# Second fold ahead of the third in the setup, and new orders for the last tiles of a cross-attention and FFN kernel

## The chip, the cores and the metric

One core of a Trainium2 chip. The metric is the device time of one execution in microseconds. The core has five engines, each with an instruction queue that is worked off in order: TensorE (PE), VectorE (DVE), ScalarE (ACT), GpSimd (POOL) and SyncE (SP), which here only issues transfers. They wait for each other by semaphores alone.

## The reference

x is 64 sequences of 64 tokens, width 256; ctx is 64 x 64 x 64. Everything is float32.

```python
q_big = einsum('bshk,hkq->bshq', (layernorm(x) @ Wq.T), w_kc_q)
kv_rope = kv_c * cos + rotate_half(kv_c) * sin
scores = (q_big . W_qr) . (kv_rope . W_kr)            # 16 heads, 64 wide
ctx_c = softmax(scores) @ kv_rope
x = x + (ctx_c . w_kc_kv) @ Wo.T
h = gelu(bitlinear(layernorm(x), w1))                 # 256 -> 1024
x = x + bitlinear(h, w2)                              # 1024 -> 256
```

bitlinear divides a row by its norm, rounds it to 8 bits by the row's largest absolute value, and multiplies it with a weight rounded to -1, 0 and 1.

## The kernel before, in words

The 4096 tokens are 32 tiles (`NT`) of 128 tokens. Setup folds the weights of queries and keys of each head into one 256 x 64 matrix: `first_fold` (W_qr with w_kc_q, PSUM banks 2 and 3, copied by `t_out`), `second_fold` (with W_kr, banks 4 and 5, `DB`, copied by `d_out`), `third_fold` (with Wq, copied by `at_out`), then `turn_a`, transposes whose result is split into `ah` and `al` by `a_hi` and `a_lo`. Each fold is made in two halves. `fold_out` does the same for w_kc_kv and Wo. Float32 products are made of three matmuls of high and low parts.

The main loop `for n in range(ENDS)` is a software pipeline written out for each engine: in step n TensorE makes `scores` of tile n, `queries` of later tiles, `shifts`, `contexts` of tile n-1, `project` of tile n-3, `up` (first FFN matmul) of tile n-7 and `down` (second) of tile n-10. VectorE finds the maxima (`quadrant_max`, `row_max`) and sums (`row_sum`, `row_inverse`) of the softmax, `divide`s the contexts, adds `residual`, and ends with `finish`. ScalarE does `exp`, `ctx_hi`, `gelu` and the squares. GpSimd does `ctx_lo`, `centre`, `x_round`, `g_round` and the small steps of the norms (`norms`, later `late_norm`). `g_round(t)` scales and rounds the 1024 gelus of a tile to integers in bfloat16 in two instructions (the first adds a large number, the second takes it away); `g_scale(t)` on VectorE gives its scale, and `turn_g(t)` on SP's queue transposes the result by DMA for `down`. `x_round` and `turn_x` do this for `up`. The inverses of the row sums go to DRAM and back, spread over partitions (`rinv_rows`, `rinv_spread`), before `divide` can use them.

After the loop, from about 355 us on, the order of the last tiles is written out by hand, one list for each engine. There `finish_late` adds the result into `xs` and `store_in_place` stores from it; `finish` writes to a buffer `yo` first. `g_round` of tiles 25, 26, 28 and 31 is done by VectorE (`DVE_LATE`), the others by GpSimd. `free_bank` makes TensorE wait until a bank that `USES` deals out in turn has been read.

## Time and profile before

| | us |
|---|---|
| three runs | 409.55, 409.83, 412.76 |
| median | 409.83 |
| profiled execution: its time | 411.0 |
| profiled execution: its span | 409.2 |
| TensorE busy in the span | 377.2 (92%) |
| VectorE, GpSimd, ScalarE busy | 319.1, 273.1, 260.4 |
| mean granted TensorE clock | 0.982 of full speed |

The span runs from the first to the last instruction of the profiled execution; its own time is 1.8 us longer and 1.2 us above the median. Instants below are microseconds from the span's start.

### The profile page before, as it was taken

The page shows a single profiled execution, that of the slowest core. Times are in us where ns is not written, and L with a number is a line of the kernel's source. Part 1 is how long each engine was busy: PE and PEld are TensorE (multiplying, and loading weights), DVE is VectorE, ACT ScalarE, POOL GpSimd, SP SyncE. Part 2 cuts the span into 40 slices and gives each one's busy share as a digit, 9 for nine tenths or more (in the row PEclk, how much of TensorE's full clock was granted, in tenths as well). Part 3 has the DMA queues.
Part 4 walks back from the last instruction along what each step waited for, and adds up shares of the span by engine and source line. Part 5 has one row for each costly group of instructions (what it writes and reads, how often), then busy time and mean ns, then how long its engine had stood idle before and what let it go on. Part 6 is the DMA issues. An engine that isn't in the chain of part 4 may idle for free.

```text
span 409.2 us, 8876 instructions
## 1 busy us (share of the span) xinstructions
PE 377.2 (92%) x2870; PEld 270.5 (66%) x2870; DVE 319.1 (78%) x669; ACT 260.4 (64%) x480; POOL 273.1 (67%) x406
## 2 busy tenths in 40 slices
PE   7898898988999999999999999999999999888764
PEld 6577656666766677777776767676767676554522
DVE  0453868779979898878797888788888888898983
ACT  1245365443586868686868686868686868667850
POOL 1026807476576787878785868686777757687882
PEclk9999999999999999999999999999999999998967
...
GB/s 201 354 377 167 106 157 128 133 129 120 104 19 84 63 105 81 117 81 99 100 93 105 78 120 71 126 67 131 69 131 66 87 111 114 103 110 148 76 96 136
DMA packets 65549, 48.75 MB, mean 119 GB/s; under 512 B 50400, under 2 KB 55904, under 8 KB 65120
## 3 DMA queue, kind: packets, MB, share of 16 engines
...
## 4 chain that ended last, share of the span: by engine, by line
POOL 47%; issue 27%; PE 9%; DMA 8%; DVE 6%; SPq 2%; POOLq 1%; ACT 0%; DVEq 0%
POOL cl L478 12%; POOL tq L504 6%; POOL qb L508 6%; POOL yc L489 3%; POOL xn L314 3%; POOL fw L527 3%; POOL xa L494 3%; DMA xs<-x 3%; DMA qt<-qb 2%; POOL xq L497 2%; PE hps L969 2%; POOL scl L534 2%; POOL rstd L216 2%; POOL fw L524 1%; PE ps L951 1%
## 5 line engine op out<-in xcount | busy, mean ns | idle before, releaser
L478 POOL TENSOR_TENSOR cl<-cr,ch 128x512 fp32r<-128x512 f32 x64 | 81.6, 1297 | 77.3 <-ACT ch L656 77.3
L640 ACT ACTIVATE qf<-ps 128x512 f32<-128x512 f32 x64 | 38.2, 596 | 71.0 <-PE ps L852 71.0
L850 PE MATMUL ps<-xh,ah 128*128 128x256 f32 x256 | 74.8, 292 | 0.3 <-ACT qf L640 0.3
L852 PE MATMUL ps<-xh,al 128*128 128x256 f32 x256 | 71.2, 278 | 0.0
L851 PE MATMUL ps<-xl,ah 128*128 128x256 f32 x256 | 71.2, 278 | 0.0
L915 PE MATMUL hps<-bh,ch 128*128 128x256 f32 x224 | 66.3, 296 | 0.0
L916 PE MATMUL hps<-bl,ch 128*128 128x256 f32 x224 | 62.6, 279 | 0.0
L917 PE MATMUL hps<-bh,cl 128*128 128x256 f32 x224 | 62.6, 279 | 0.0
L850 PEld LDWEIGHTS ps<-xh,ah 128*128 128x128 f32 x256 | 48.1, 188 | 17.1 <-issue 16.2
L656 ACT ACTIVATE ch<-cr 128x512 fp32r<-128x512 f32 x64 | 39.3, 632 | 24.0 <-DVE cr L1184 23.9
L1151 DVE TRANSPOSE_TENSOR_REDUCE red<-hps 128x16 f32<-128x512 f32 x64 | 41.8, 690 | 13.0 <-PE hps L867 12.9
L851 PEld LDWEIGHTS ps<-xl,ah 128*128 128x128 f32 x256 | 48.1, 188 | 0.0
L852 PEld LDWEIGHTS ps<-xh,al 128*128 128x128 f32 x256 | 48.1, 188 | 0.0
L682 ACT ACTIVATE g<-ps,scl 128x512 f32<-128x512 f32 x64 | 40.8, 682 | 10.1 <-PE ps L951 9.9
L1184 DVE TENSOR_TENSOR cr<-ps,rb 128x512 f32<-128x512 f32 x64 | 41.3, 685 | 6.9 <-issue 4.3
L951 PE MATMUL ps<-w1q,xqt 128*128 128x512 bf16 x128 | 37.5, 396 | 7.5 <-DMA xqt<-xq 6.1
L915 PEld LDWEIGHTS hps<-bh,ch 128*128 128x128 f32 x224 | 42.2, 189 | 1.4
L1158 DVE TRANSPOSE_TENSOR_REDUCE red<-pe 128x16 f32<-128x512 f32 x64 | 41.6, 688 | 1.8 <-ACT pe L651 1.8
L916 PEld LDWEIGHTS hps<-bl,ch 128*128 128x128 f32 x224 | 42.2, 188 | 0.3
L917 PEld LDWEIGHTS hps<-bh,cl 128*128 128x128 f32 x224 | 42.3, 189 | 0.0
L1206 DVE TENSOR_REDUCE amax<-g 128x1 f32<-128x1024 f32 x32 | 38.7, 1208 | 0.9 <-ACT g L682 0.8
L651 ACT ACTIVATE pe<-hps 128x512 f32<-128x512 f32 x64 | 34.6, 596 | 7.2 <-PE hps L895 7.2
...
## 6 DMA issues: line engine op xcount, KB each, us to landing
...
```

The lines of the kernel that those rows point to most:

```text
L478: pool.tensor_tensor(cl[:, u % 2, :, b * S:(b + 1) * S], cr[:, :, b * S:(b + 1) * S], ch[:, u % 2, :, b * S:(b + 1) * S].bitcast(F32), ALU ...
L682: act.activation(g[:, t % GB, 512 * half:512 * half + 512], turn_bank("h", t, half), ACT.Gelu, scale=hscale(scl, t)).then_inc(sem["gelu_do ...
L850: pe.matmul(o, ah[:, c, cols], xh[:, k % 2, c, :], start=(c == 0), stop=False)
L851: pe.matmul(o, ah[:, c, cols], xl[:, k % 2, c, :], start=False, stop=False)
L852: m = pe.matmul(o, al[:, c, cols], xh[:, k % 2, c, :], start=False, stop=(c == KC - 1))
L915: pe.matmul(O[:, 0:D], c_h, bh[:, hp, :], start=(hp == 0), stop=False)
L916: pe.matmul(O[:, 0:D], c_h, bl[:, hp, :], start=False, stop=False)
L917: m = pe.matmul(O[:, 0:D], c_l, bh[:, hp, :], start=False, stop=(hp == HP - 1))
L951: m = pe.matmul(turn_bank("h", t, half), xqt[:, t % 2, c, :], w1q[:, c, 512 * half:512 * half + 512], start=(c == 0), stop=(c == KC - 1))
L1151: dve.tensor_reduce(red[:, u % 2, 16 * b:16 * b + 16], SB[b].rearrange("p (k s) -> p k s", s=32), AX.X, ALU.max, apply_transpose=True).the ...
L1158: dve.tensor_reduce(red[:, (u + 1) % 2, 64 + 16 * b:80 + 16 * b], pe32[:, u % 2, b, :].rearrange("p (k s) -> p k s", s=32), AX.X, ALU.add, ...
L1184: dve.tensor_tensor(cr[:, :, b * S:(b + 1) * S], CB[b].rearrange("p (h s) -> p h s", s=S), rb[:, b, :].rearrange("p (h s) -> p h s", s=S), ...
```

## The change

1. Setup. TensorE makes the second half of `second_fold` ahead of the first half of `third_fold`, with three idle matmuls in front. `turn_a(0)` and `(1)` write banks 4 and 5 in place of the two that the queries use. VectorE copies `d_out(0)` before the statistics of the first x tiles, and converts `em` and takes the statistics of tiles 4 to 7 later. SP loads the second x part and `em_s` only once the first fold is made.
2. Stores. `finish` writes to `xs` too; `yo` is only room now.
3. End. No `g_round` is done by VectorE; tiles 25 and 31 go to ScalarE, and 26 and 28 to GpSimd besides its own six. `ctx_lo(31)` and `x_round(28)` move from GpSimd to VectorE, `centre(30)` from ScalarE to GpSimd. The lists of all five engines are written anew.

TensorE in the setup, before and after; `wkr_s,t_s` is the second fold, `wq_s,d_s` the third, `ident,at_s` the turning:

```order
L985 MATMUL ps<-wk_b,wqr_b 64x128 x2
L1007 MATMUL hps<-wq_s,d_s 64x256 x8
L326 MATMUL ps<-ident,xn 128x128 x4
L996 MATMUL hps<-wkr_s,t_s 128x64 x8
L1019 MATMUL ps<-ident,at_s 128x128 x8
```

```order
L996 MATMUL ps<-wk_b,wqr_b 64x128 x2
L986 MATMUL hps<-ones 128x128 x3
L1010 MATMUL hps<-wkr_s,t_s 128x64 x8
L1021 MATMUL hps<-wq_s,d_s 64x256 x8
L325 MATMUL ps<-ident,xn 128x128 x4
L1034 MATMUL hps<-ident,at_s 128x128 x8
```

The fold with W_kr has moved over the one with Wq and over the transposes of x.

VectorE at the start of the end (`cr<-ps,rb` is `divide`, `ri<-rs` is `row_inverse`, `amax<-g` is `g_max`), before and after:

```order
L1151 TENSOR_REDUCE red<-hps 128x16 x2
L1184 TENSOR_TENSOR cr<-ps,rb 128x8x64
L1164 TENSOR_REDUCE nmax<-hps 32x64
L1170 TENSOR_REDUCE rs<-hps 32x64
L1184 TENSOR_TENSOR cr<-ps,rb 128x8x64
L1189 SCALAR_TENSOR_TENSOR xs,xsum<-hps,xs 128x256
L1177 RECIPROCAL ri<-rs 32x64
```

```order
L1167 TENSOR_REDUCE red<-hps 128x16 x2
L1228 TENSOR_REDUCE amax<-g 128x1
L1180 TENSOR_REDUCE nmax<-hps 32x64
L1233 SCALAR_TENSOR_TENSOR gm<-amax,level 128x1
L1235 RECIPROCAL c_73<-gm 128x1
L1211 SCALAR_TENSOR_TENSOR xs,xsum<-hps,xs 128x256
L1186 TENSOR_REDUCE rs<-hps 32x64
L1216 TENSOR_REDUCE amax<-yc 128x1 x2
L1222 SCALAR_TENSOR_TENSOR gm<-amax,level 128x2
L1224 RECIPROCAL c_64<-gm 128x2
L1200 TENSOR_TENSOR cr<-ps,rb 128x8x64 x2
```

Both halves of `divide(29)` now stand behind nine instructions that stood behind them, or behind the first half.

ScalarE around its first `g_round`, after (`g,magic,c_73` and `qb<-g,magic`; `ch<-cr` is `ctx_hi(31)`):

```order
L679 ACTIVATE g<-ps,scl 128x512
L685 ACTIVATE sqj,stat<-g 128x1024 x2
L692 ACTIVATE g<-g,magic,c_73 128x1024
L696 ACTIVATE qb<-g,magic 128x1024
L653 ACTIVATE ch<-cr 128x8x64 x2
```

`ctx_hi(31)` stands behind the two new instructions of tile 25.

The diff, with most of the lists of the end left out:

```diff
-POOL_LATE = (22, 23, 24, 27, 29, 30)
-DVE_LATE = (25, 26, 28, 31)
+POOL_LATE = (22, 23, 24, 26, 27, 28, 29, 30)
+ACT_LATE = (25, 31)
...
-        yo = sb("yo", [P, 2, D], F32, at)
+        sb("room", [P, 2, D], F32, at)
...
-        USES = [("k", 0), ("e",), ("x", 0), ("a", 0), ("a", 1), ("q", 0, 0), ("q", 0, 1), ("x", 1), ("q", 0, 2), ("q", 0, 3)]
+        USES = [("k", 0), ("e",), ("x", 0), ("q", 0, 0), ("q", 0, 1), ("x", 1), ("q", 0, 2), ("q", 0, 3)]
...
-                if kind == "a":
-                    pe.wait_ge(sem["a_lo_done"], a + 1)
 
         FB, DB, AT = bank[2:4], bank[4:6], [bank[6], bank[7], bank[2], bank[3]]
 
         def turned_a(q):
-            return turn_bank("a", q) if q < 2 else (T, O)[q - 2]
+            return (DB[0], DB[1], T, O)[q]
...
-                    sp.dma_start(out[:, t, :], yo[:, t % 2, :]).then_inc(sem[f"out_stored{t % 2}"], 16)
-
-                def store_in_place(t):
-                    sp.wait_ge(sem["outputs"], t + 1)
...
+                sp.wait_ge(sem["t_made"], 2)
+                load_x(1)
                 for b in range(2):
                     sp.dma_start(em_s[64 * b:64 * b + 64, :], consts[b:b + 64, 2 * DC + b * P:2 * DC + (b + 1) * P]).then_inc(sem["em_loaded"], 16)
-                load_x(1)
-                sp.wait_ge(sem["t_made"], 2)
...
+                turn_x(26)
                 rinv_rows(30)
                 rinv_spread(30)
-                turn_x(26)
-                store_in_place(21)
-                turn_g(23)
+                store(21)
                 rinv_rows(31)
                 turn_x(27)
-                store_in_place(22)
+                turn_g(23)
+                store(22)
                 rinv_spread(31)
                 turn_g(24)
-                store_in_place(23)
+                store(23)
+                turn_x(28)
                 turn_g(25)
-                turn_x(28)
                 turn_x(29)
+                store(24)
                 turn_g(26)
-                store_in_place(24)
+                store(25)
+                turn_x(30)
                 turn_g(27)
-                turn_x(30)
                 turn_x(31)
+                store(26)
                 turn_g(28)
-                store_in_place(25)
-                store_in_place(26)
+                store(27)
                 turn_g(29)
-                store_in_place(27)
+                store(28)
                 turn_g(30)
-                store_in_place(28)
+                store(29)
                 turn_g(31)
-                store_in_place(29)
-                store_in_place(30)
-                store_in_place(31)
+                store(30)
+                store(31)
...
-                    last = t - 1 if t < POOL_LATE[0] + 1 else POOL_LATE[POOL_LATE.index(t) - 1]
+                    last = t - 1 if t < 22 else (21, *POOL_LATE)[POOL_LATE.index(t)]
                     pool.wait_ge(sem["g_scale_steps"], 2 * (t + 1))
                     if last >= 0:
                         pool.wait_ge(sem[f"g_rounded{last % 2}"], last // 2 + 1)
                     pool.tensor_scalar(tq[:, :], g[:, t % GB, :], c2[:, t:t + 1], MAGIC, ALU.mult, ALU.add).then_inc(sem["g_scaled"], 1)
-                    pool.wait_ge(sem["g_scaled"], t + 1 if t < POOL_LATE[0] else POOL_LATE[0] + POOL_LATE.index(t) + 1)
+                    pool.wait_ge(sem["g_scaled"], t + 1 if t < 22 else 23 + POOL_LATE.index(t))
...
+                late_norm(1, 13)
+                x_round(26)
+                late_norm(0, 13)
                 ctx_lo(29, 0)
                 ctx_lo(29, 1)
-                x_round(26)
-                late_norm(0, 13)
                 g_round(23)
                 centre(29)
-                late_norm(1, 13)
                 g_round(24)
+                late_norm(0, 14)
                 ctx_lo(30, 0)
                 ctx_lo(30, 1)
-                x_round(28)
+                late_norm(1, 14)
                 x_round(29)
-                late_norm(0, 14)
-                ctx_lo(31, 0)
-                ctx_lo(31, 1)
-                late_norm(1, 14)
+                centre(30)
+                g_round(26)
+                late_norm(1, 15)
                 g_round(27)
-                late_norm(1, 15)
                 late_norm(0, 15)
+                g_round(28)
+                g_round(29)
                 late_norm(1, 16)
-                g_round(29)
...
+                def g_round(t):
+                    gt = g[:, t % GB, :]
+                    act.wait_ge(sem["magic_set"], 2)
+                    act.wait_ge(sem["g_scale_steps"], 2 * (t + 1))
+                    act.wait_ge(sem["g_squared"], t + 1)
+                    act.activation(gt, gt, ACT.Identity, scale=c2[:, t:t + 1], bias=magic[:, 0:1]).then_inc(sem["g_raised_act"], 1)
+                    act.wait_ge(sem["g_raised_act"], ACT_LATE.index(t) + 1)
+                    act.wait_ge(sem[f"g_rounded{t % 2}"], t // 2)
+                    act.wait_ge(sem[f"gqt_turned{t % 2}"], 16 * (t // 2))
+                    act.activation(qb[:, t % 2, :], gt, ACT.Identity, bias=magic[:, 1:2]).then_inc(sem[f"g_rounded{t % 2}"], 1)
+
...
+                d_out(1)
                 at_out(0)
                 x_hi(act, 0)
-                d_out(1)
...
+                centre(28)
+                square_x(28)
                 ctx_hi(29, 0)
                 ctx_hi(29, 1)
-                centre(28)
-                square_x(28)
                 exp(31, 0)
                 exp(31, 1)
                 gelu(24, 0)
                 gelu(24, 1)
                 square_g(24)
+                gelu(25, 0)
+                gelu(25, 1)
                 square_x(29)
-                gelu(25, 0)
+                gelu(26, 0)
                 ctx_hi(30, 0)
-                gelu(25, 1)
+                ctx_hi(30, 1)
+                gelu(26, 1)
                 square_g(25)
-                ctx_hi(30, 1)
-                gelu(26, 0)
-                gelu(26, 1)
                 square_g(26)
-                gelu(27, 0)
+                g_round(25)
                 ctx_hi(31, 0)
                 ctx_hi(31, 1)
+                gelu(27, 0)
                 gelu(27, 1)
+                square_x(30)
                 square_g(27)
-                centre(30)
-                square_x(30)
+                centre(31)
+                square_x(31)
                 gelu(28, 0)
                 gelu(28, 1)
+                gelu(29, 0)
                 square_g(28)
-                centre(31)
-                square_x(31)
-                gelu(29, 0)
...
+                g_round(31)
...
+                    if u == 0:
+                        pe.wait_ge(sem["a_lo_done"], 2)
...
+                    if hh == 1:
+                        pe.wait_ge(sem["d_act"], 1)
+                        pe.wait_ge(sem["d_dve"], 1)
...
-                    if q < 2:
-                        free_bank(pe, "a", q)
+                    if q == 0:
+                        pe.wait_ge(sem["d_act"], 2)
+                        pe.wait_ge(sem["d_dve"], 2)
...
+                idle(O, 3)
+                second_fold(1)
                 third_fold(0)
                 x_t(pe, 0)
-                second_fold(1)
...
+                shifts(31)
                 contexts(30)
                 project_high(29)
-                shifts(31)
+                turned(32)
+                down_late(21)
+                up(25, 0)
                 project_low(29)
-                down_late(21)
+                up(25, 1)
                 down_late(22)
-                turned(32)
-                up(25, 0)
-                up(25, 1)
                 up(26, 0)
-                down_late(23)
+                up(26, 1)
                 contexts(31)
-                up(26, 1)
-                project_high(30)
                 up(27, 0)
                 up(27, 1)
...
+                def ctx_lo(u, b):
+                    dve.wait_ge(sem["ctx_hi"], 2 * u + b + 1)
+                    dve.wait_ge(sem["projected"], u - 1)
+                    dve.tensor_tensor(cl[:, u % 2, :, b * S:(b + 1) * S], cr[:, :, b * S:(b + 1) * S],
+                                      ch[:, u % 2, :, b * S:(b + 1) * S].bitcast(F32), ALU.subtract).then_inc(sem["ctx_lo"], 1)
+
...
                     dve.wait_ge(sem[f"xqt_turned{t % 2}"], 16 * (t // 2))
                     dve.tensor_scalar(xq[:, t % 2, :], xa[:, :], 1.0, -MAGIC, ALU.mult, ALU.add).then_inc(sem["x_rounded"], 1)
 
-                def g_round(t):
-                    gt = g[:, t % GB, :]
-                    dve.wait_ge(sem["g_scale_steps"], 2 * (t + 1))
-                    dve.wait_ge(sem["g_squared"], t + 1)
-                    dve.tensor_scalar(gt, gt, c2[:, t:t + 1], MAGIC, ALU.mult, ALU.add).then_inc(sem["g_raised"], 1)
-                    dve.wait_ge(sem["g_raised"], DVE_LATE.index(t) + 1)
-                    dve.wait_ge(sem[f"g_rounded{t % 2}"], t // 2)
-                    dve.wait_ge(sem[f"gqt_turned{t % 2}"], 16 * (t // 2))
-                    dve.tensor_scalar(qb[:, t % 2, :], gt, 1.0, -MAGIC, ALU.mult, ALU.add).then_inc(sem[f"g_rounded{t % 2}"], 1)
-
                 def finish(t):
                     dve.wait_ge(sem["products"], t + 1)
                     dve.wait_ge(sem["norm_steps"], norm_count(t // 2 + 2))
-                    at_least(dve, sem[f"out_stored{t % 2}"], 16 * (t // 2))
-                    dve.scalar_tensor_tensor(out=yo[:, t % 2, :], in0=O[:, D:2 * D], scalar=gscale(scl, t),
+                    dve.scalar_tensor_tensor(out=xs[:, t, :], in0=O[:, D:2 * D], scalar=gscale(scl, t),
                                              in1=xs[:, t, :], op0=ALU.mult, op1=ALU.add).then_inc(sem["outputs"], 1)
 
                 def finish_late(t):
...
-                statistics(dve, 0, 4)
                 d_out(0)
                 dve.wait_ge(sem["end_made"], 1)
                 dve.tensor_copy(kvt[:, KR - 1, :], turn_bank("e")[:, 0:P]).then_inc(sem["end_copied"], 1)
+                statistics(dve, 0, 4)
+                d_out(1)
                 at_out(0)
                 x_lo(dve, 0)
-                d_out(1)
                 a_lo(0)
                 a_lo(1)
-                dve.wait_ge(sem["em_loaded"], 32)
-                dve.tensor_copy(em[:, :], em_s[:, :]).then_inc(sem["em_set"], 1)
                 at_out(1)
-                statistics(dve, 4, 6)
                 a_lo(2)
                 a_lo(3)
                 x_lo(dve, 1)
-                statistics(dve, 6, 8)
+                dve.wait_ge(sem["em_loaded"], 32)
+                dve.tensor_copy(em[:, :], em_s[:, :]).then_inc(sem["em_set"], 1)
+                statistics(dve, 4, 8)
...
+                g_max(23)
+                row_max(31)
+                g_scale(23)
+                residual(28)
+                row_sum(30)
+                x_max(27)
+                x_max(28)
+                x_scale(13)
                 divide(29, 0)
-                row_max(31)
-                row_sum(30)
                 divide(29, 1)
-                residual(28)
+                x_round(27)
                 row_inverse(30)
-                x_max(27)
-                x_scale(13)
-                x_max(28)
-                g_max(23)
-                g_scale(23)
-                x_round(27)
                 quadrant_sum(31, 0)
                 quadrant_sum(31, 1)
-                finish_late(21)
-                residual(29)
                 row_sum(31)
                 row_inverse(31)
+                finish_late(21)
                 g_max(24)
-                divide(30, 0)
...
```

## Rows read from the trace of the kernel before

**Rows 1.** The page: busy us of the engines, granted clock in 40 slices.
```profile
PE 377.2 (92%) x2870; PEld 270.5 (66%) x2870; DVE 319.1 (78%) x669; ACT 260.4 (64%) x480; POOL 273.1 (67%) x406
...
PEclk9999999999999999999999999999999999998967
```

**Rows 2.** Windows: stretch and its length, then busy time of each engine, clock, DMA.
```profile
60.00:350.00 290.00, 281.89 (x2182) 205.10 (x2182) 243.08 (x513) 203.84 (x370) 209.01 (x307) 1.00 0.41 98
```

**Rows 3.** Timeline, 19 to 25 us: start, duration, engine, line; in brackets the wait.
```profile
19.50 0.60 ACT L704 ACTIVATE t_s<-ps 128x512 f32<-128x512 f32 x1 [3.06 <-PE ps L985]
...
20.15 1.95 PE L1007 MATMUL hps<-wq_s,d_s 128*64 128x256 f32 x16 [0.70 <-DMA wq_s<-wq]
...
22.14 0.69 DVE L1285 COPY at_s<-hps 128x512 f32<-128x512 f32 x1 [2.23 <-PE hps L1007]
...
23.16 1.11 PE L996 MATMUL hps<-wkr_s,t_s 64*128 64x64 f32 x16
...
24.20 1.10 PE L1019 MATMUL ps<-ident,at_s 128*128 128x128 f32 x8
```

**Rows 4.** Timeline, 33 to 47 us.
```profile
33.90 0.19 POOL L213 TENSOR_SCALAR nw<-mv 128x4 f32<-128x4 f32 x1 [9.47 <-DVE mv L204]
...
43.56 2.06 POOL L314 TENSOR_SCALAR xn<-xs,rstd,nmean 128x256 f32<-128x256 f32 x2
...
46.58 0.60 PE L326 MATMUL ps<-ident,xn 128*128 128x128 f32 x4
```

**Rows 5.** Timeline, 356 to 370 us: VectorE, GpSimd, SyncE's queue.
```profile
356.73 0.65 DVE L1184 TENSOR_TENSOR cr<-ps,rb 128x512 f32<-128x512 f32 x1
...
358.99 2.52 POOL L478 TENSOR_TENSOR cl<-cr,ch 128x512 fp32r<-128x512 f32 x2
...
363.57 1.30 SPq L359 DMA_DIRECT2D rb<-rinv_d  x2
...
369.56 0.69 DVE L1184 TENSOR_TENSOR cr<-ps,rb 128x512 f32<-128x512 f32 x1 [1.21 <-issue]
```

**Rows 6.** Windows of 1 us around the first fall of the clock.
```profile
368.00:369.00 1.00, 0.00 (x0) 0.00 (x0) 0.36 (x1) 1.00 (x3) 0.81 (x3) 1.00 0.81 89
...
370.00:371.00 1.00, 0.48 (x3) 0.09 (x2) 0.96 (x5) 0.71 (x2) 0.37 (x1) 0.76 0.82 168
...
373.00:374.00 1.00, 1.00 (x8) 0.03 (x4) 1.00 (x2) 0.77 (x2) 1.00 (x1) 0.54 0.35 135
```

**Rows 7.** Groups by line and shape from 355 us on: count, busy us, mean ns, idle.
```profile
L1206 DVE TENSOR_REDUCE amax<-g 128x1 f32<-128x1024 f32 x9 | 10.9, 1210 | 0.9 <-ACT g L682 0.8
...
L504 POOL TENSOR_SCALAR tq<-g,c 128x1024 f32<-128x1024 f32 x7 | 7.8, 1116 | 2.5 <-DVE c L1213 2.1 <-POOL qb L508 0.2
...
L508 POOL TENSOR_SCALAR qb<-tq 128x1024 bf16<-128x1024 f32 x7 | 7.3, 1045 | 0.6
...
L547 POOL TENSOR_TENSOR fw<-fw,mhalf 128x2 f32<-128x2 f32 x8 | 6.0, 756 | 0.7
...
L1231 DVE TENSOR_SCALAR qb<-g 128x1024 bf16<-128x1024 f32 x4 | 3.9, 972 | 0.6 <-DMA qt<-qb 0.5
...
L1227 DVE TENSOR_SCALAR g<-g,c 128x1024 f32<-128x1024 f32 x4 | 3.8, 962 | 0.0
...
L1211 DVE SCALAR_TENSOR_TENSOR gm<-amax,level 128x1 f32<-128x1 f32 x9 | 3.1, 344 | 0.1
...
L688 ACT ACTIVATE sqj<-g 128x1024 bf16<-128x1024 f32 x8 | 8.5, 1058 | 0.3
```

**Rows 8.** Timeline, 383 us to the end.
```profile
383.17 1.20 PE L932 MATMUL hps<-bh,cl 128*128 128x256 f32 x8
...
389.30 0.29 DVE L1221 TENSOR_SCALAR xq<-xa 128x256 bf16<-128x256 f32 x1
...
402.29 1.24 SPq L369 DMA_TRANSPOSE qt<-qb  x1
...
405.42 1.05 PE L969 MATMUL hps<-w2q,qt 128*128 128x256 bf16 x8 [0.83 <-DMA qt<-qb]
```

56 lines of the change are left out of this document (31 added, 25 removed).

## The prediction

> **What bounds the kernel now.** I read the page first, for shares: TensorE is busy 377.2 of 409.2 us and its clock is full in all but the last three slices [rows 1]. Then the windows by stage, since one share over three stages says little: from 60 to 350 us TensorE is busy 281.9 of 290 us, 97% [rows 2]. Nothing in that stage is shortened, and its one edit is where `finish` writes, so whatever the setup gains or loses passes through it one to one, and it gives nothing itself. What is left are the setup and the last 54 us, where the order lists decide. There I read the timeline, for who is late at each hand-over.
>
> **Setup.** Before, the third fold starts at 20.15 after a wait of 0.70 for the query weights; transposes of x and the late second fold stand behind it, and the turning starts at 24.20, as soon as the second fold (23.16, some 1.1) has gone through the engine. VectorE's copy of the third fold had ended at 22.8 (22.14 plus 0.69), 1.4 us earlier [rows 3]. Now the second fold runs first. It needs ScalarE's copy `t_out(1)`, which starts at 19.50 and lasts 0.60, so it starts at 20.15, the very time at which the third fold used to start. Third fold: 21.2 to 23.15. x transposes fill the time of the copies; VectorE's copy runs 23.2 to 23.9; the turning starts at 23.95. Gain: 24.20 - 23.95 = 0.25, taken as **0.2**. The weights now may land 1.05 us later at no cost. The wait for `d_dve` is no new one: `d_out(0)` now stands ahead of the statistics. The idle matmuls run in the wait for `t_out(1)`; without that cover three cost some 0.5.
>
> Three moves of the setup I cost at nothing. SP: x part 2, two `em_s` pieces and w1 are issued after the first fold, so w1 goes out about 1.5 us later than before, and the first reader of w1 on ScalarE comes only after the second `x_hi`, well behind the landing. VectorE: statistics of tiles 4 to 7 come later, behind `x_lo(1)` and `em`, so GpSimd's `reciprocal_deviations(1)`, which waited 9.47 us for them until 33.90, starts some 0.8 later. What hides it: its pair of x normalisations took 2.06 from 43.56, and TensorE takes them at 46.58, 0.96 after their end [rows 4]. If that cover is gone, it costs at most the 0.8. The bound for the setup is thus a gain of 0.4 to a loss of 0.8. Banks 4 and 5 for the turning make `scores(0)` wait for `a_lo(1)`, done long before.
>
> **Stores.** `finish` into `xs` has the same shape; its old wait for the buffer goes, and SP still stores it. I cost it at nothing, both ways: VectorE is not what TensorE waits for there.
>
> **The end, step by step** (instants of the old trace, the 0.2 not yet taken off).
> (1) VectorE. `divide(29)` ran at 356.73 [rows 5]. Now `g_max(23)` (1.21 [rows 7]) and ten small instructions come first, among them `residual(28)`, which waits for TensorE's `project_low(28)` until about 358.9. `divide(29)` runs 360.9 to 362.2. GpSimd's `ctx_lo(29)` follows at 363.7, after two late norms and `x_round(26)` that were moved ahead of it (a late norm is a chain of four, the longest 0.76 [rows 7]; I count 1.7 for one). Before it ran at 358.99 [rows 5]: it is 4.7 later.
> (2) TensorE has `shifts(31)` directly ahead of `contexts(30)` and must wait for the shift rows until 361.2, then for `divide(29)` until 362.2: 2.9 idle out of 3.4. Before, a wait of like length ended in a fall of the clock: nothing ran at 368 to 369, the clock averaged 0.76 at 370 to 371 and was at 0.54 still at 373 to 374 [rows 6], so 1.2 GHz in place of 2.4 from about 370.8 until shortly before 374. I take a fall of the same length here, which makes `contexts(30)` and `project_high(29)` end at 366.8, in place of 365.3 at full clock.
> (3) `row_inverse(30)` ends at 363.3. Its trip through DRAM: spread issued at 365.5, where it was at 363.57; the old divide got it at 369.56, 6.0 after that issue [rows 5]; so 371.5, and with `finish_late(22)` ahead of it 371.8. `divide(30)` is **2.2 late**.
> (4) From here time comes back. VectorE is rid of four g rounds: 3.8 + 3.9 = 7.7 us [rows 7], and takes `ctx_lo(31)` (two subtractions, 0.7 each) and `x_round(28)` (0.7), 2.1; net 5.6 less. ScalarE takes two g rounds. The nearest row is its squaring of a tile of the same 128x1024, 1.06 [rows 7]; I take 1.1 an instruction and 2.2 a tile, bounds 2.1 and the 2.2 that GpSimd needs (1.12 + 1.05). The first ends at 379.2, and `ctx_hi(31)` stands behind it on its engine; `divide(31)` ends at 379.7 anyway, since its spread is issued behind `turn_g(23)` and `store(22)`. `project_high(31)` 380.5 to 382.5, `project_low(31)` to 383.7: before 383.17 plus 1.20, 384.4 [rows 8]. Now 0.7 ahead.
> (5) `residual(31)`, centring, `x_max(31)`, `x_scale(15)`, two x rounds: done at 388.3, before 389.6 (389.30 plus 0.29 [rows 8]). 1.3 ahead.
> (6) GpSimd: rounds 26, 27, 28, 29 and 30 at 2.2 each with the norms between; round 29 ends at 394.3, round 30 at 398.2. ScalarE has `gelu(31)` by 395.1, VectorE gives its scale at 397.6, ScalarE rounds until 399.9.
> (7) SP: `turn_g(30)`, `store(29)`, then `turn_g(31)` at 400.2, before 402.29; the last `down` follows 3.1 later, as it did (405.42), and the span ends as before, 6.9 after that issue [rows 8]. The end gains **2.1**.
>
> The Trainium skill (ScalarE: Activation LUTs, "What ACT_TABLE_LOAD costs") gives 280 ns plus 0.833 ns a column for an ACTIVATE with a pointer as bias, by which the two of a tile are an estimated 2.3 to 2.4 us and the sum would be 0.1 to 0.2 smaller. No table is loaded for them in the new order, and the trace shows none for the centring on ScalarE.
>
> **Sum.** 0.2 + 0 + 2.1 = 2.3. The profiled span of 409.2 becomes 406.9, its time 411.0 would be 408.7; against the median of the runs, which lies 1.2 below that execution, **409.83 - 2.3 = 407.5**.
>
> **Rivals.**
> (a) The clock stays full at 362 us. For it: `shifts(31)` breaks the idle time; against: a piece of `up` did so before too. Steps 3 to 7 then come 0.9 earlier: 3.0 + 0.2 off, 406.6.
> (b) GpSimd hardly waits. In my steps it waits 3.6 us after 363.7; its work alone (30.9 us: eight g rounds less one, two `ctx_lo`, six norms, the small ones) would end at 394.6. If `divide(30)` comes back sooner than the old trip says, up to that much more: 403.9 at best, typically 405.
> (c) Slower: the 4.7 of `ctx_lo(29)` is carried one to one, as `project_low(29)`, `residual(29)` and `finish_late(22)` stand ahead of `divide(30)` on VectorE. Then `divide(30)` starts at 374.3, 2.5 later than in my steps, and all behind it: 407.5 + 2.5 + up to 1 for a second fall of the clock = 411. It decides at 374.1, where the 2.3 are used up. Against it: the trip through DRAM does not depend on TensorE.
> (d) Last `g_scale`s wait for GpSimd. On VectorE this instruction does one column, and still takes 0.344 on average in the end, more than twice what the reciprocals beside it need, so some of the nine wait [rows 7]. GpSimd now has two rounds more there. If scale 31 and one before it on the path wait for a running half of a round (1.1): 408.6. The Trainium skill (SBUF — State Buffer, "Who interferes with whom") says that an instruction of VectorE with two SBUF inputs waits for a reading one of GpSimd, for its full length; the trace agrees, and by that page `ctx_lo(31)` on VectorE is of this kind too.
> (e) The setup's part turns round, by the late statistics: 407.5 + 1.0 = 408.5.
>
> **Chances.** My steps 0.45; (a) 0.17; (b) 0.14; (c) 0.10; (d) 0.09; (e) 0.05. The predicted time is that of the likeliest. A measurement of this kernel tells about 1% from no change: 405.7 and 413.9. Below 405.7 lies nearly all of (b) and a small part of (a) and of my steps: 0.19. Above 413.9 only the tail of (c): 0.03. Within: 0.78. The range leaves out the best end of (b) and the worst of (c): 404.4 to 410.3.
>
> **What would show it.** Right: the turning at about 23.9 and the last matmul of the span's end near 406.9; `divide(30)` near 371.6, the last x round near 388, the last `turn_g` near 400. Half clock at 362 to 366 shows step 2. Wrong: `divide(30)` behind 374 (c); `gm` of tiles 28 to 31 at over 1 us (d); GpSimd with no idle row after 370 (b); the first `scores` later than before (e).

## The result: 0.5% slower, and the profile after

On one chip, 20 executions each in turn: before 411.5 us, the change **414.54 us**, ratio **1.0053** (95%: 1.0033 to 1.0073), that is 1.4 to 3.0 us slower. The forecast was 407.5, 2.3 faster. The profiled execution of the change has a span of 413.0 us and a time of 414.9, against 409.2 and 411.0.

The page of the change first: busy times, and the granted clock in 40 slices, as in [rows 1].

```profile
PE 378.3 (92%) x2861; PEld 275.2 (67%) x2876; DVE 315.4 (76%) x665; ACT 264.6 (64%) x483; POOL 271.6 (66%) x409
...
PEclk9999999999999999999999999999999999969987
```

VectorE is 3.7 us less busy and ScalarE 4.2 more, as the change intends. The clock row dips in slice 36 of 40; before, the first dip was in slice 37, and shallower [rows 1].

The setup, timeline of the change, beside [rows 3]:

```profile
18.84 0.60 ACT L712 ACTIVATE t_s<-ps 128x512 f32<-128x512 f32 x1 [2.91 <-PE ps L996]
19.59 1.11 PE L1010 MATMUL hps<-wkr_s,t_s 64*128 64x64 f32 x16
20.63 1.95 PE L1021 MATMUL hps<-wq_s,d_s 128*64 128x256 f32 x16
...
23.46 1.07 PE L1034 MATMUL hps<-ident,at_s 128*128 128x128 f32 x8 [0.29 <-DVE at_s L1296]
```

The turning starts at 23.46 in place of 24.20: 0.7 sooner. The first scores keep it: 34.9 in place of 35.6. One execution of each can't show that the edits gave it: in the profiles of this study whose clock row has no dip in the setup, the first scores start between 33.8 and 36.1 with the new setup (14 profiles), and at 35.3 and 35.6 with the old one.

The long middle, window from 60 to 350 us as in [rows 2], and two groups of its product matmuls (count, busy us, mean ns), of the change and then of before:

```profile
60.00:350.00 290.00, 282.46 (x2168) 207.56 (x2174) 241.44 (x508) 202.40 (x367) 208.35 (x307) 1.00 0.39 97
```
```profile
L927 PE MATMUL hps<-bl,ch 128*128 128x256 f32 x224 | 63.0, 281 | 0.0
...
L861 PE MATMUL ps<-xh,al 128*128 128x256 f32 x216 | 60.6, 281 | 0.0
```
```profile
L916 PE MATMUL hps<-bl,ch 128*128 128x256 f32 x224 | 62.6, 279 | 0.0
...
L852 PE MATMUL ps<-xh,al 128*128 128x256 f32 x216 | 60.1, 278 | 0.0
```

Same shapes, same clock of 1.00, same code for them, and each of these matmuls is 2 to 3 ns longer (the groups of 64x512, 613 to 615 ns, are not). From the first scores to the last it takes 319.2 us in place of 317.7: 1.5 us lost in a stage in which no order was changed.

The end, first TensorE, then the windows of the clock fall, then VectorE:

```profile
356.55 0.36 PE L937 MATMUL hps<-bh,ch 128*128 128x256 f32 x1 [0.41 <-DVE xs L1248]
...
361.94 0.49 PE L906 MATMUL hps<-shift,em 64*128 64x512 f32 x2 [2.19 <-DMA shift<-nmax]
...
363.19 1.08 PE L916 MATMUL ps<-pe,kvn 64*64 64x512 f32 x1 [0.76 <-DVE cr L1200]
```
```profile
362.00:363.00 1.00, 0.43 (x2) 0.12 (x2) 1.00 (x3) 0.52 (x1) 0.90 (x3) 0.87 1.09 248
363.00:368.00 5.00, 4.80 (x21) 3.23 (x22) 2.45 (x6) 4.94 (x8) 4.63 (x6) 0.50 0.12 32
368.00:370.00 2.00, 2.00 (x14) 1.70 (x13) 0.83 (x2) 0.44 (x2) 1.30 (x2) 0.61 0.85 225
370.00:373.00 3.00, 2.95 (x23) 2.36 (x22) 2.20 (x8) 1.51 (x3) 0.64 (x2) 1.00 0.15 46
```
```profile
361.76 1.29 DVE L1200 TENSOR_TENSOR cr<-ps,rb 128x512 f32<-128x512 f32 x2
...
369.14 0.29 DVE L1186 TENSOR_REDUCE rs<-hps 32x64 f32<-32x128 f32 x1 [3.59 <-PE hps L892]
...
373.40 1.28 DVE L1200 TENSOR_TENSOR cr<-ps,rb 128x512 f32<-128x512 f32 x2
...
381.51 1.29 DVE L1200 TENSOR_TENSOR cr<-ps,rb 128x512 f32<-128x512 f32 x2 [1.65 <-DMA rb<-rinv_d]
...
383.86 2.94 DVE L1206 TENSOR_TENSOR cl<-cr,ch 128x512 fp32r<-128x512 f32 x2
...
390.29 0.84 DVE L1240 TENSOR_SCALAR xa<-yc,c 128x256 f32<-128x256 f32 x1
391.16 1.10 DVE L1243 TENSOR_SCALAR xq<-xa 128x256 bf16<-128x256 f32 x1
...
392.79 0.29 DVE L1243 TENSOR_SCALAR xq<-xa 128x256 bf16<-128x256 f32 x1
```

TensorE stands 2.19 us ahead of `shifts(31)` and 0.76 ahead of `contexts(30)`, 2.95 together. Then the clock is at 0.50 (1.2 GHz) in all of 363 to 368, and by the means of the windows beside it (0.87 and 0.61) from 362.7 to 369.6: seven microseconds, with TensorE busy. VectorE waits 3.59 for the turned sums behind that slow stretch, and the later divides carry it. The three L1200 rows are `divide(29)`, `(30)` and `(31)`; L1206 is `ctx_lo(31)`, and L1240 and L1243 are the last two x rounds.

And the last stretch, where [rows 8] are the rows of before: SyncE's queue, ScalarE's round of g 31, the end of GpSimd's round of g 30, TensorE.

```profile
402.24 0.34 SPq L372 DMA_DIRECT2D out<-xs  x1
403.66 1.25 SPq L368 DMA_TRANSPOSE qt<-qb  x1
404.95 0.57 SPq L372 DMA_DIRECT2D out<-xs  x1
405.62 1.24 SPq L368 DMA_TRANSPOSE qt<-qb  x1
```
```profile
402.79 1.24 ACT L692 ACTIVATE g<-g,magic,c 128x1024 f32<-128x1024 f32 x1 [1.35 <-DVE c L1235]
404.06 1.15 ACT L696 ACTIVATE qb<-g,magic 128x1024 bf16<-128x1024 f32 x1
```
```profile
402.59 1.04 POOL L503 TENSOR_SCALAR qb<-tq 128x1024 bf16<-128x1024 f32 x1
```
```profile
406.47 1.33 PE L980 MATMUL hps<-w2q,qt 128*128 128x256 bf16 x8 [3.05 <-DMA qt<-qb]
408.41 1.89 PE L980 MATMUL hps<-w2q,qt 128*128 128x256 bf16 x8 [0.61 <-DMA qt<-qb]
```

I call what lies from the start of `project_high(28)` to the end of the span **the tail**: 53.46 us before (from 355.74), 56.45 in the change (from 356.55). So by the traces: setup -0.7, middle +1.5, tail +3.0, sum 3.8, the difference of the two spans. The medians differ by 3.0, at the upper end of what the interval allows.

Inside the tail the change takes 36.5 us to the end of the last x round (before 33.9), from there 12.5 to the start of the last `turn_g` (before 12.7), and 7.4 behind it (before 6.9). So against the kernel before, nearly all of the tail's loss stands ahead of the last x round, and none between it and the last `turn_g`.

### The profile page after: what moved, and what is told of

It reads as the page before. It is cut to its first block, busy times and chain, and to the rows that moved or that the text cites. A ratio compares the mean times of both kernels' runs of the same rounds, so it can differ in the third digit from the quotient of the medians.

```text
span 413.0 us, 8878 instructions
## 1 busy us (share of the span) xinstructions
PE 378.3 (92%) x2861; PEld 275.2 (67%) x2876; DVE 315.4 (76%) x665; ACT 264.6 (64%) x483; POOL 271.6 (66%) x409
## 4 chain that ended last, share of the span: by engine, by line
PE 68%; DVE 9%; issue 6%; DMA 6%; POOL 5%; SPq 3%; ACT 2%; POOLq 0%; ACTq 0%; DVEq 0%
PE ps L859 7%; PE ps L861 6%; PE ps L860 6%; PE hps L926 6%; PE hps L878 6%; PE ps L916 6%; PE hps L928 6%; PE hps L927 6%; PE ps L962 5%; PE hps L972 5%; DMA kv_s<-kv 2%; PE hps L906 2%; DMA rb<-rinv_d 2%; DVE cr L1200 2%; PE ps L325 1%
## 5 line engine op out<-in xcount | busy, mean ns | idle before, releaser
L473 POOL TENSOR_TENSOR cl<-cr,ch 128x512 fp32r<-128x512 f32 x62 | 78.7, 1290 | 78.0 <-ACT ch L653 78.0
L1200 DVE TENSOR_TENSOR cr<-ps,rb 128x512 f32<-128x512 f32 x64 | 41.2, 686 | 5.9 <-DMA rb<-rinv_d 3.6
L962 PE MATMUL ps<-w1q,xqt 128*128 128x512 bf16 x113 | 33.4, 389 | 5.3 <-ACT g L679 2.2
L878 PE MATMUL hps<-qf,kvt 64*64 64x512 f32 x256 | 34.8, 613 | 3.6 <-ACT pe L648 2.9
```

Of the source, the lines that this page charges most:

```text
L473: pool.tensor_tensor(cl[:, u % 2, :, b * S:(b + 1) * S], cr[:, :, b * S:(b + 1) * S], ch[:, u % 2, :, b * S:(b + 1) * S].bitcast(F32), ALU ...
L878: m = pe.matmul(SB[b][dst, :], kvt[src, (u - gg) % KR, b * L:(b + 1) * L], qf[src, k % 2, :, cols], start=True, stop=False, skip_group_che ...
L962: m = pe.matmul(turn_bank("h", t, half), xqt[:, t % 2, c, :], w1q[:, c, 512 * half:512 * half + 512], start=(c == 0), stop=(c == KC - 1))
L1200: dve.tensor_tensor(cr[:, :, b * S:(b + 1) * S], CB[b].rearrange("p (h s) -> p h s", s=S), rb[:, b, :].rearrange("p (h s) -> p h s", s=S), ...
```

## The experiments

Every kernel was timed in five rounds beside the kernel before on the same chip; ratios are to it. Where the granted clock decides, I also give the median of the executions whose mean clock was 0.998 or more ("at full clock"). Theories have letters in the expectations: A, setup gains and end loses; C, the half clock behind `shifts(31)`; D, the later contention and the late spread; M, a displacement of the tiles in SBUF lengthens matmuls, N, it doesn't; G, GpSimd is the bound; later ones are explained where they stand.

### One part alone

`e1_setup`: the kernel before with the setup's edits and `finish` into `xs`. `e2_end`: the change with the old setup.

> The kernel before with the setup's part of the change and the stores from xs, and the old lists of the end. The changed kernel turned its matrices at 23.46 us where the one before did at 24.20 (I had counted 0.25 for the order itself; the rest was a first fold that came earlier). Theory A (the setup gains, the end loses): 0.2 to 0.7 us faster than before, ratio 0.998 to 0.9995. Rival B (the setup's moves cost something later in the program, since the changed kernel had lost 1.4 us between 35 and 355 us): 0.5 to 1.5 us slower, ratio 1.001 to 1.004.

> The changed kernel with the old setup: the new lists of the end and the stores from xs alone. Theory A: it carries the whole loss, 2.4 to 3 us slower than before (the changed kernel's ratio of 1.0053 is 2.2 us, plus what the setup had given), ratio 1.0055 to 1.0075. Rival B: about 1 us slower, ratio 1.001 to 1.004.

Measured: 410.73 us, ratio 0.9984 (0.9955 to 1.0013), tail 53.6; and 414.77 us, 1.0073 (1.0044 to 1.0101), tail 55.9. Both are what theory A said. I take the setup to be worth some 0.7 us: three signs agree (the turning, e1, and e2 against the change), but each is within its own noise. The loss comes with the end's edits, of which the new tile `magic` is one.

### The clock, and the head of the end

`e3_idle` is the change with idle matmuls in the two waits; `e5_head` has the first section of each engine's list as before.

```
                 project_low(28)
+                pe.wait_ge(sem["residuals"], 29)
+                idle(O, 6)
                 shifts(31)
+                idle(O, 4)
                 contexts(30)
```

> The changed kernel with idle matmuls where TensorE waits at 360 to 363 us: six after the residual of tile 28, four between the shifts and the contexts of tile 30. Their results are read by nothing. Theory C (the clock that stood at half from 362.1 to 369.2 us is what made the end late): the clock stays at 1.00 there, the high part of the projection of tile 29 takes 1.9 us in place of 3.8, the divide of tile 30 comes about 1.3 us earlier, and the kernel is 0.8 to 2 us faster than the changed one: ratio to before 1.000 to 1.004. Rival D (the end is late by what comes after, the contention of the subtraction of tile 31 and the late spread): the clock stays full, and the time falls by less than 0.5 us, ratio 1.004 to 1.0055.

> The changed kernel with the first section of each engine's list at the end (up to the second half of tile 31's sums) as it was before: divide of tile 29 right behind the maxima of tile 31, contexts and projection ahead of the shifts, the subtraction of tile 29 on GpSimd ahead of the norms. Theory C: TensorE has no wait of over 1 us at 360 us, the clock stays full, the divide of tile 30 starts 3 to 4 us sooner than in the changed kernel, and the kernel is 2 to 4 us faster than the changed one, ratio to before 0.996 to 1.001. Rival D: the later part alone costs what was lost; the gain over the changed kernel is under 1.5 us, ratio 1.002 to 1.0055.

`e3_idle`: 412.99 us, 1.0029 (1.0006 to 1.0052). Its windows:

```profile
360.00:370.00 10.00, 9.95 (x76) 7.97 (x78) 8.00 (x21) 8.30 (x15) 8.68 (x15) 1.00 0.43 99
370.00:375.00 5.00, 3.62 (x25) 1.68 (x24) 4.58 (x10) 4.52 (x9) 4.19 (x7) 1.00 0.59 154
```

The clock stays at 1.00 there, and the tail is 54.5 instead of 56.45. That the waits bring the half clock is shown. Its price is 2.0 us by the two traces and 1.0 by the ratios, whose intervals overlap. `e5_head`: 413.75, 1.0071 (1.0041 to 1.0102), tail 56.9. Neither theory's number:

```profile
372.85 0.48 DVE L1257 SCALAR_TENSOR_TENSOR xs<-hps,scl,xs 128x256 f32<-128x256 f32 x1 [2.20 <-POOL scl L546]
373.25 1.28 DVE L1200 TENSOR_TENSOR cr<-ps,rb 128x512 f32<-128x512 f32 x2
```

`finish_late(22)` now waits for a norm that GpSimd has behind its centring, and `divide(30)` queues behind it. Counted from the tail's start it comes 1.1 us sooner than in the change, where theory C asked for 3 to 4, and TensorE waits there (3.07); the clock averages 0.72 from 372 to 376. The wait had mostly moved, by my own mix of two orders; this run says nothing for or against the head.

### Sixty-four bytes

`magic`, new in the change, is 8 bytes a partition and moves all that is allocated behind it by 64. `e9_pad` is the kernel before plus one unused tile; `e10_place` is the change with `magic` in room already allocated.

```
         mhalf = sb("mhalf", [P, 4], F32)
+        sb("pad", [P, 2], F32)
```

> The kernel before with one unused tile of 8 bytes (64 with its alignment) where the changed kernel has its tile of constants, so that every later tile lies 64 bytes further on; no instruction differs. In all four profiles of kernels with that tile the matmuls of queries and projection took 281 ns on average, in both without it 278 to 280, and the stage from 35 to 355 us was 1.4 us longer. Theory M (the place in memory slows the matmuls): 281 ns here too, 1 to 2 us slower than before, ratio 1.0025 to 1.005. Rival N (it is another thing of those kernels, or chance): 278 to 280 ns, ratio within 0.0015 of 1.

> The changed kernel with its tile of constants laid in room that nothing uses, so that every tile has the address that it has in the kernel before. Theory M: 278 to 280 ns a matmul, and 1 to 2 us faster than the changed kernel, ratio to before 1.001 to 1.003. Rival N: 281 ns and the ratio of the changed kernel, 1.0045 to 1.006.

`e9_pad`, then `e10_place`, product matmuls of the middle:

```profile
L916 PE MATMUL hps<-bh,ch 128*128 128x256 f32 x218 | 64.9, 298 | 0.0
L851 PE MATMUL ps<-xh,ah 128*128 128x256 f32 x216 | 63.5, 294 | 0.0
```
```profile
L926 PE MATMUL hps<-bh,ch 128*128 128x256 f32 x224 | 66.2, 296 | 0.0
L859 PE MATMUL ps<-xh,ah 128*128 128x256 f32 x216 | 62.8, 291 | 0.0
```

An unused tile gives the old kernel the change's durations (298 and 294 ns for 296 and 291), and taking the displacement out of the change gives them back. First scores to last: 317.2 to 318.6 us in the 13 profiles of this study with the old addresses, 319.0 to 320.9 in the 7 with the new. So M is shown for the durations and the middle. As a time it is not: `e9_pad` took 412.06, 1.0004 (0.9974 to 1.0033), which is N's number; of its lost 3 us in the middle 2.3 came back in a tail of 51.1 whose clock fell later. `e10_place` took 413.2, 1.0039 (1.0003 to 1.0074), 0.6 below the change and between the theories. Below it is measured with the clock held.

### ctx_lo(31) back to GpSimd, and idle matmuls in the old end

`e6_lo_idle`: `e3_idle` with `ctx_lo(31)` on GpSimd again. `e8_old_idle`: the setup part with the **old** end, and idle matmuls in five of its waits.

```
+                pe.wait_ge(sem["rinv_steps"], 63)
+                idle(T, 9)
                 up(26, 0)
...
+                idle(T, 14)
                 up(30, 0)
...
+                idle(T, 9)
                 down_late(29)
+                idle(T, 3)
                 down_late(30)
+                idle(T, 3)
                 down_late(31)
```

> The changed kernel with the ten idle matmuls of the earlier run and the two subtractions of tile 31 given back to GpSimd, ahead of its g round 26. On VectorE the two took 2.94 us beside GpSimd's g round of tile 26 in place of some 1.3. If that contention is what the end still loses (theory D): TensorE's low part of tile 31 starts 0.5 to 1 us sooner, g_max of tile 27 2.5 us sooner, and the kernel is 0.5 to 1.5 us faster than the run with the idle matmuls alone (1.0029): ratio 0.9995 to 1.002. If GpSimd is the bound of the end (rival G), its 2.5 us more of work are paid there: ratio 1.003 to 1.007.

> The kernel with the new setup and the old lists of the end, and idle matmuls where TensorE waits there: nine ahead of the first FFN matmuls of tile 26, fourteen ahead of those of tile 30, and nine, three and three ahead of the last three products. Their results are read by nothing. If the half clock in the waits of the end costs time by itself (theory C): clock 1.00 to the end, FFN matmuls of tiles 30 and 31 in 2.1 us in place of 3.8, and 0.8 to 2 us faster than with the new setup alone (0.9984): ratio 0.9935 to 0.9965. Rival: the end goes by GpSimd, ScalarE and transfers, and the clock is hidden: within 0.4 us of it, ratio 0.9975 to 0.9995; slower, if the idle matmuls stand in the way.

`e6_lo_idle`: 412.78, 1.0021 (0.9991 to 1.0052), no clear gain over `e3_idle`. Its tail was 52.7, 1.8 shorter, but the clock too stayed full for longer there: its clock row dips in the last slice alone, that of `e3_idle` in the last two. `e8_old_idle`: **408.56 us, ratio 0.9919 (0.9887 to 0.9952)**, clock 1.00 in every slice, tail 51.4. It beats both kernels. Against `e1_setup`, the same without the idle matmuls, it is 2.2 us by the medians and 2.7 by the ratios, on two chips. So the old end too was losing to the clock, which my sum took as given.

### Both ends with the clock held

> The kernel before with idle matmuls in three waits of its end, nothing else changed; against the same with the setup part (408.6 us, 51.4 us tail) it prices the setup part with the clock held. Theory A (the setup part gains what its trace shows at the first scores, 0.7): 409.2 to 409.6, ratio 0.993 to 0.994 to the kernel before. Rival (the gain is caught up before the end): 408.4 to 408.8, ratio 0.991 to 0.992.

> Setup part, old end, idle matmuls (408.6 us) and one unused tile of 8 bytes a partition, which moves what is allocated behind it by 64 bytes. Theory M (the displacement lengthens each 128x256 and 128x512 matmul by 2 to 3 ns, and with the clock held nothing hides it): matmul means 281 instead of 278, scores to scores 319.5 to 321, time 1.5 to 3 us more than without the tile: 410.1 to 411.6, ratio 0.995 to 0.999. Rival N (the longer means are a record's matter and the time is the clock's luck): within 0.5 us of 408.6, ratio 0.991 to 0.993.

> The change with magic's 64 bytes in unused room (addresses as before) and idle matmuls in every stall of TensorE longer than half a microsecond from project_high(28) on, so that the clock should be granted in full to the end; ctx_lo(31) stays on VectorE. The reference for it is the same treatment of the old end (setup part, old end, idle matmuls), which gave 408.6 us with a tail of 51.4. Theory F (in the end the change lost only by the clock and by ctx_lo(31)): tail 52.0 to 52.6 (the old 51.4 and 0.7 to 1.2 for ctx_lo(31) beside GpSimd), 409.0 to 409.8. Rival K (the new orders are late in themselves, by divide(30) and divide(31)): tail 53.5 or more, 410.5 or more, and moving ctx_lo(31) does not bring it under 53.

> As the run before it in this batch, with ctx_lo(31) back on GpSimd, ahead of its round of g 26. Theory D (two-input subtractions on VectorE beside the rounding GpSimd cost 1.5 us, most of which TensorE sees): 0.7 to 1.3 us faster than with VectorE's, project_low(31) waited for 0.3 to 0.6 us instead of 1.2. Rival (TensorE has room behind it, as down_late waits for the turned g anyway): within 0.4 of it. Theory F: 408.3 to 409.0, level with the old end at full clock; rival K: 410 or more.

| kernel | all, us | ratio (95%) | at full clock | tail of the profile |
|---|---|---|---|---|
| e8: setup part, old end | 408.56 | 0.9919 (0.9887 to 0.9952) | 408.1 (7 of 10) | 51.4 |
| e13: old setup, old end | 412.0 | 0.9988 (0.9955 to 1.0020) | 410.6 (4 of 12) | 51.8 |
| e14: e8 and 64 bytes | 410.0 | 0.9930 (0.9898 to 0.9961) | 409.7 (10 of 12) | 51.0 |
| e11: new end, ctx_lo(31) on VectorE | 411.4 | 0.9982 (0.9950 to 1.0014) | 411.3 (10 of 12) | 53.2 |
| e12: the same on GpSimd | 411.34 | 0.9967 (0.9938 to 0.9995) | 411.2 (9 of 12) | 53.7 |

The 64 bytes (e14 against e8) cost 1.6 us by the medians at full clock, but 0.5 by the ratios, on two chips and inside the intervals. The trace of e14 has M's matmuls and M's middle (319.7 us), and a tail 0.4 shorter than that of e8; the price in the whole time stays open between 0.5 and 1.6.

The place of `ctx_lo(31)` shows no price (D falls). The traces show where it went: in e12 `project_low(31)` ends 0.6 sooner after the tail's start than in e11, but the last x round only 0.4 sooner, as one x round takes 1.11 and 1.10 us beside GpSimd's rounding (0.84 and 1.10 in e11, 0.35 and 0.29 in the kernel before), and behind it `turn_g(28)` takes 4.7 us to land, in e11 4.0.

And **the new end is 3.1 us slower than the old one with the clock full in both** (e11 against e8, on two chips whose kernel before took 412.1 on either; 2.6 by the ratios, 1.8 by the tails; 1.5 against e14, which ran on the same chip and carries the 64 bytes). F, the clock alone, falls; K, the orders are late in themselves, is the nearer, though its tail was to be 53.5 or more. Against the kernel before, e11 and e12 (0.9982 and 0.9967) have no loss left, while the change has 1.0053 (1.0033 to 1.0073), above both of their intervals: the clock and the addresses together are the whole loss, and the late orders are why nothing was gained.

e13 puts the setup at 2.4 us, over three times its trace, and neither of its theories' numbers came. Its profile had the clock down in the setup, and over all its executions it is not clearly faster than the kernel before (0.9988), though its tail is 1.7 shorter. That figure stays open, and I keep 0.7.

### What in the new drain

`e18_fewer` is `e11_full_dve` with fewer idle matmuls ahead of the last two products, the control. `e15_scale31` exchanges `g_scale(31)` and `finish_late(28)` on VectorE; `e16_dve31` and `e17_dve28` also round g 31, and g 28 too, on VectorE:

```
                 g_max(31)
-                finish_late(28)
                 g_scale(31)
+                finish_late(28)
```

> Control for the three that follow: the change with the addresses of before and idle matmuls in the stalls of its end, 9 and 2 of them ahead of the last two down products instead of 12 and 3, so that they can hide no gain there. Every theory: 410.5 to 411.5 us, clock 0.99 to 1.00, last down product 49.4 us behind the start of project_high(28), as with 12 and 3.

> The control with two instructions of VectorE's list exchanged: g_scale(31) ahead of finish_late(28), which waits for the product of tile 28, as in the kernel before. Theory Q (the last round of g is late because its scale stands behind that wait): g_scale(31) at the end of g_max(31) instead of 1.5 to 2.4 us later, ScalarE's round of g 31 that much sooner, then GpSimd's round of g 30 is the later one: 1.0 to 2.0 us faster than the control. Rival U (the end is set by GpSimd's rounds of 29 and 30 and the norms between them): 0 to 0.4.

> As the run before, and the round of g 31 on VectorE right behind its scale, none by ScalarE: what VectorE's missing round costs at the very end. Theory R (ScalarE's 2.4 us against VectorE's 1.5 is on the path): 0.5 to 0.9 faster than with the exchange alone. Rival U: within 0.3 of it, as round 30 by GpSimd lands as late.

> As the run before, and the round of g 28 on VectorE too, behind its scale, so that GpSimd has rounds 29 and 30 alone behind 27, as in the kernel before. Theory U (GpSimd's 2.3 us a round are the end's pace): rounds 29 and 30 start 2.3 us sooner, 1.0 to 2.0 faster than the run before, level with the old end (408 to 409). Rival (the g maxima and x rounds on VectorE are then late by the 1.5 us that it takes on): within 0.5.

At full clock: 411.3 (12 of 12), 410.7 (10), 413.0 (7), 412.6 (7); the ratios are 0.9963, 0.9977, 1.0034 and 1.0038. The exchange gave 0.6 by these medians and nothing by the ratios, where theory Q asked for 1.0 to 2.0. ScalarE in `e15_scale31`:

```profile
398.68 1.24 ACT L692 ACTIVATE g<-g,magic,c 128x1024 f32<-128x1024 f32 x1 [0.72 <-DVE c L1248]
401.23 1.15 ACT L696 ACTIVATE qb<-g,magic 128x1024 bf16<-128x1024 f32 x1 [1.31 <-DMA qt<-qb]
```

Its round starts 1.5 sooner after the tail's start than in the control, and its second half then waits 1.31 for `turn_g(29)` to free the buffer. `e16_dve31` was my mistake: `finish_late(28)` stood behind that round, `store(28)` waits for it, and on SyncE's queue `turn_g(30)` stands behind the store: it went out at 406.8, though GpSimd had rounded g 30 by 405.3. In `e17_dve28`, built on it, GpSimd's round 29 waited 4.33 for its scale, as its rival said. `e20_dve31` takes this out again, with VectorE's round behind `finish_late(28)`; `e19_norm_first` adds round 28 on VectorE and the norm of 28 and 29 ahead of GpSimd's rounds 29 and 30:

> The control with VectorE's list g_max(31), g_scale(31), finish_late(28), g_round(31), as in the kernel before, no round of g 31 on ScalarE: VectorE's round on its own, without the wait that the last batch's version put ahead of turn_g(30). Theory R (ScalarE's 2.4 us for the last round against 1.5 are on the path): 0.5 to 1.2 faster than the control's 411.3, 410.1 to 410.8. Rival U (GpSimd's round of 30, ending 44.7 us behind the start of project_high(28), sets turn_g(30) and with it the end): 410.8 to 411.3.

> As the run before, with round 28 on VectorE behind g_scale(29), the norm of tiles 28 and 29 ahead of GpSimd's rounds 29 and 30 instead of between them, and finish_late(27) behind g_scale(30). Theory U (GpSimd's queue, rounds 28, 29, norm, 30 in a row, is the pace of the drain): its round of 30 ends 0.8 to 1.4 sooner, 0.7 to 1.4 faster than the run before. Rival (VectorE's 1.5 us for round 28 puts g_max(30) and g_scale(30) back by as much): within 0.3 of it, GpSimd waits for g_scale(30).

411.4 (6 of 12) and 411.7 (9 of 12), ratios 0.9989 and 1.0000, on another chip than the control: no gain from either, where R asked for 0.5 to 1.2 and U for 0.7 to 1.4. GpSimd and SyncE's queue in `e20_dve31`:

```profile
398.51 1.04 POOL L502 TENSOR_SCALAR qb<-tq 128x1024 bf16<-128x1024 f32 x1
```
```profile
399.81 0.34 SPq L371 DMA_DIRECT2D out<-xs  x1
400.25 1.24 SPq L367 DMA_TRANSPOSE qt<-qb  x1
401.80 0.34 SPq L371 DMA_DIRECT2D out<-xs  x1
402.23 1.24 SPq L367 DMA_TRANSPOSE qt<-qb  x1
```

g 30 is rounded at 399.55, but `turn_g(30)` goes out at 400.25, behind `store(28)`, and so behind product 28, which had waited until 398.21. It is not so in the change: its round 30 ends at 403.63, `turn_g(30)` goes out at 403.66, and `store(28)` had gone out at 402.24. In the old end with the clock held, `e8_old_idle`:

```profile
390.84 1.25 SPq L367 DMA_TRANSPOSE qt<-qb  x1
...
394.74 1.24 SPq L367 DMA_TRANSPOSE qt<-qb  x1
...
397.17 1.24 SPq L367 DMA_TRANSPOSE qt<-qb  x1
...
399.13 1.24 SPq L367 DMA_TRANSPOSE qt<-qb  x1
```

`turn_g(28)` goes out 3.1 us after the last x round (387.77), lands after 3.1, and the store that waits for product 28 stands ahead of `turn_g(31)` alone; it went out at 398.46, when that product had been done since 395.0. In `e20_dve31` `turn_g(28)` goes out 3.9 after the last x round, and lands 5.3 later (398.21). In all new drains at the old addresses (e10 to e12, e15 to e20) the slowest landing took 3.8 to 5.3 us; in the change, e2, e3 and e5 3.6, in e6 2.8; in the old drains (before, e1, e8, e9, e13, e14) never over 3.4.

The new list of SyncE has each of these stores one turn further ahead: `store(28)` stands in front of `turn_g(30)`, where the old list has `store(27)`. In e12, e15, e16, e19 and e20, turn, product, `finish_late`, `store` and the next turn are one chain, by which `turn_g(30)` goes out 0.1 to 1.5 us after its round has ended. In the change, e3, e6, e10, e11, e17 and e18 the two are 0.03 apart, and GpSimd's round sets it. That the place of the stores costs time is argued: no run moves the stores alone. Why the landing is longer I have not shown. Closeness of what follows does not explain it: `turn_g(29)` of e8 has `store(27)` 1.3 and `turn_g(30)` 2.4 behind it and lands after 3.1, `turn_g(28)` of e20 has its followers 1.4 and 2.6 behind it and needs 5.3.

## Why the forecast was wrong, by its own steps

The sum said 2.3 faster, and the trace is 3.8 slower, 6.1 apart. Of this the middle is 1.5, costed at nothing; the tail is 5.1, forecast at 2.1 gained and measured at 3.0 lost; the setup gave 0.5 back. Two steps brought most of it: the stores and the middle, where I put a new tile at nothing, and step (2), where the half clock is mis-sized, with `divide(31)` in step (4), which stands behind it. What is left are the contention in (4) and (5) and the rounds in (6).

Instants of the change's trace, less 0.81 (it enters the tail that much later), against the steps:

| step | forecast | change | e11, clock held |
|---|---|---|---|
| (1) divide(29) starts | 360.9 | 360.95 | 360.96 |
| (2) TensorE's wait | 2.9 | 2.95 | filled |
| (3) divide(30) starts | 371.8 | 372.6 | 370.4 |
| (4) divide(31) ends | 379.7 | 382.0 | 379.2 |
| (4) project_low(31) ends | 383.7 | 387.3 | 384.5 |
| (5) last x round ends | 388.3 | 392.3 | 389.5 |
| (6) GpSimd's round 30 ends | 398.2 | 402.8 | 400.0 |
| (7) turn_g(31) | 400.2 | 404.8 | 402.0 |

(The last column is moved onto the same scale by +0.85.)

**Setup**: right in direction, 0.7 for 0.2. The order of the folds ran as said, but the chain began 0.6 sooner, since ScalarE's copy came at 18.84 and not at 19.50. That may be luck: with the old setup the copy came at 18.76 in `e9_pad`, with the new one at 17.75 in `e3_idle` and 20.01 in `e18_fewer`.

**Stores and the middle**: the step that failed unseen. I costed the edits at nothing and did not look at what the new tile `magic` moves. It lengthens the 1320 matmuls of 128x256 in that window by 2 to 3 ns each (they overlap, so this doesn't add up), and the middle by 1.5 us in this trace, by 2.2 between the means of the 13 and of the 7 profiles.

**(1) and (2), the wait**: right to 0.1 us. **(2), the clock**: failed in size. I took a fall as long as the old one, which by the means of [rows 6] was 3.4 us, from 370.5 (not 370.8) to 373.9; this one lasted seven, with TensorE busy in it. `project_high(29)` ended at 368.1 on this scale, not 366.8, and with it the turned sums that `row_inverse(31)` waits for.

**(3)** only 0.8 late. What came last ahead of it was not the trip through DRAM but `finish_late(22)`, whose product ended at 372.96: the wait of rival (c), at a third of its price. **(4), divide(31)**: failed, 2.3 late. Its row inverses wait for the sums (3.59), and its trip waits on SyncE for `store(21)`, whose product also stood in the slow stretch: `rinv_rows(31)` goes out at 371.28, then `turn_x(27)`, `turn_g(23)` and `store(22)` back to back, the spread at 375.52, and it takes the 6.0 us that the old one took. "Issued behind them anyway" left out that the whole queue was late. With the clock held (e11) `divide(31)` ends 0.5 ahead of the forecast, so its lateness was the clock's.

**(4), ctx_lo(31)**: failed by 1.5. I priced two subtractions at 0.7 each; they took 2.94 together. GpSimd's halves of round 26 run beside them, from 383.70 for 1.13 and from 384.91 for 1.35. If each subtraction waited for the half beside it and then ran its 0.7, they would end at 385.5 and 387.0; they ended at 385.4 and 386.8. The Trainium skill (SBUF — State Buffer, "Who interferes with whom") says that an instruction of VectorE with two SBUF inputs contends with one of GpSimd that reads SBUF; the trace agrees. I had cited this place of the Trainium skill in rival (d), and left the price at 0.7. That no time came back when GpSimd took it (e11 against e12) shows that a mis-sized step need not be a costly one: the gain was spent again in the x rounds and the landing behind them.

**(5)** 0.4 more. The first of the last two x rounds took 0.84 and 1.10 us, beside GpSimd's two halves of round 27 (from 389.87 for 1.11 and from 391.07 for 1.04); before, with only a norm on GpSimd, its two instructions took 0.35 and 0.29. No step counted this 1.3.

**(6) and (7)**: in the change the last turn is 4.6 behind the forecast, of which 4.0 stand already at the last x round and 0.6 more at GpSimd's round 30. Even with the clock held and the old addresses (e11) it is 1.8 behind: 1.2 at the last x round and 0.6 at round 30. Steps 6 and 7 also left out that SyncE's queue ties `turn_g(30)` to product 28 through `store(28)`, and that each landing is part of that chain; this binds in e12, e15, e16, e19 and e20, but neither in the change nor in e11. Behind the last turn the change loses 0.5 more, with its last product at half clock (1.89 for 1.05). ScalarE's round took 2.39, not 2.2. The estimate of 2.3 to 2.4 from the Trainium skill (ScalarE: Activation LUTs, "What ACT_TABLE_LOAD costs") holds.

Of the rivals, (c) came nearest in its number, for another reason: its 411 us had the divide late, at 374.3; it was 372.6, and the loss came from the clock, the middle and the contention. The sign of (d), a `gm` of over 1 us, did not come (0.79 at most, tile 29); its kind of wait came at `ctx_lo(31)`. Rival (a), the clock full, was to gain 0.9 more; with the clock held the last turn was still 1.8 late. One thing stands above all steps: I took the old end's waits as harmless. With the clock held, the old end alone puts its last `turn_g` at 400.2 on the old scale (399.13 + 1.11), which is the very instant that I forecast for the new lists.
